# Attention with relative positions and a quantised FFN: the row maxima of four query tiles turned by one transpose, in front of the weighing matmuls

## The reference

```python
q, k, v = heads(ln(x) @ Wq + bq), heads(ln(x) @ Wk + bk), heads(ln(x) @ Wv + bv)   # (4*12, 1024, 16)
attn = einsum('bqd,bkd->bqk', q, k) / sqrt(16)
attn = attn + rel_bias_h[..., :, None] + rel_bias_w[..., None, :]   # from q and rel_h, rel_w
attn = softmax(attn, axis=-1)                                       # 1024 queries x 1024 keys
x = x + (einsum('bqk,bkd->bqd', attn, v) as (4, 32, 32, 192)) @ Wp + bp
t = x
t = t + ffn(ln(t))   # quantise, w1, gelu, clip, quantise, w2
```

## Time and profile before

| | |
|---|---|
| median of 3 runs | 863.06 us (858.8, 863.06, 864.1) |
| profiled execution | 859.48 us |
| its span, first to last instruction | 857.7 us |
| busy, share of the span | PE 90%, DVE 80%, ACT 67%, POOL 53% |
| mean granted TensorE clock | 0.951 of full speed (1.00 in the attention) |
| L1134 DVE reductions | 384, 451.5 us busy |
| L1088 ACT exponentials | 768, 410.7 us busy |
| L1013 / L993 / L1025 PE | 264.6 / 239.1 / 204.1 us busy |
| L1093 ACT copies of the maxima | 24, 24.3 us busy, 48.0 us idle before them |

### The profile page before, as it was taken

One profiled execution on the slowest core, in us unless ns is written; L12 is line 12 of the kernel. 1 busy time (PEld: TensorE's weight loads), 2 busy tenths in 40 slices (PEclk: granted clock), 3 DMA queues, 4 the chain that ended last, 5 costly groups with the idle time before them and its releaser, 6 DMA issues. The chain is left out here.

```text
span 857.7 us, 14811 instructions
## 1 busy us (share of the span) xinstructions
PE 767.9 (90%) x5688; PEld 401.1 (47%) x5688; DVE 687.9 (80%) x929; ACT 572.6 (67%) x969; POOL 453.6 (53%) x292
## 2 busy tenths in 40 slices
PE   4969565388999999999999999999999999989975
PEld 2635365244444444444444444444444444347753
DVE  6999765398888888888888888888888888249994
ACT  1233345306877887787777887787788778868773
POOL 2577699317474664837373846557473334512330
PEclk9979878659999999999999999999999999999988
DMA  7756679999959393957769492939487120033411
GB/s 196 214 165 217 207 182 372 377 210 186 190 112 209 70 216 65 217 100 163 153 125 191 88 212 66 207 66 220 92 176 140 55 82 13 13 123 128 151 37 55
DMA packets 65750, 130.02 MB, mean 152 GB/s; under 512 B 9535, under 2 KB 45392, under 8 KB 57224
## 3 DMA queue, kind: packets, MB, share of 16 engines
q1 hardware_dynamic: 57648, 115.95, 58.5%
q10 hardware_dynamic: 8032, 13.13, 4.3%
HBM read 89.73 MB, written 34.60 MB: 145 GB/s over the span
## 5 line engine op out<-in xcount | busy, mean ns | idle before, releaser
L1134 DVE TENSOR_REDUCE at_neg_max<-at_r_ps 128x1 f16<-128x1024 f32 x384 | 451.5, 1217 | 84.7 <-PE at_r_ps L993 84.7
L1088 ACT ACTIVATE at_probs<-at_s_ps 128x512 f32<-128x512 f32 x768 | 410.7, 600 | 92.8 <-PE at_s_ps L1013 92.0
L1013 PE MATMUL at_s_ps<-op_mix_q,op_mix_k 128*128 128x512 f16 x768 | 264.6, 382 | 4.6 <-ACT at_probs L1088 1.6
L993 PE MATMUL at_r_ps<-op_mix_k,op_mix_q 128*128 128x256 f16 (+1 forms) x1920 | 239.1, 257 | 16.7 <-DMA op_mix_q<-bias_parts 12.0
L1025 PE MATMUL at_o_ps<-at_probs,op_v_u 128*32 128x512 f32 x1536 | 204.1, 604 | 0.0
L993 PEld LDWEIGHTS at_r_ps<-op_mix_k,op_mix_q 128*128 128x128 f16 x1920 | 156.8, 100 | 94.1 <-DVE at_neg_max L1134 15.8
L910 POOL COPY op_mix_q<-op_mix_q 2x4096 f16<-2x4096 f16 x48 | 171.6, 3601 | 1.5
L1013 PEld LDWEIGHTS at_s_ps<-op_mix_q,op_mix_k 128*128 128x128 f16 x768 | 74.1, 97 | 166.3 <-issue 69.6
L220 POOL MEMSET op_mix_q<- 2x10240 f32 x12 | 103.5, 8627 | 21.2 <-PE at_o_ps L1025 21.1
L914 POOL TENSOR_TENSOR at_o_sb<-at_o_sb,at_inv_rows 128x512 f32<-128x512 f32 x23 | 29.4, 1280 | 126.5 <-DVE at_inv_rows L1150 125.3
L907 POOL COPY op_mix_q<-op_mix_q 2x1024 f16<-2x1024 f16 x24 | 24.9, 1036 | 107.3 <-ACT op_mix_q L1093 107.3
(11 more groups left out here) (131 smaller groups left out, 682.0 us busy)
## 6 DMA issues: line engine op xcount, KB each, us to landing
op_mix_q<-qk_parts SPq DMA_DIRECT2D x48, 640.0 KB, 11.0
op_mix_q<-bias_parts SPq DMA_DIRECT2D x120, 120.0 KB, 9.6
op_mix_q<-bias_parts SPq DMA_DIRECT2D x72, 128.0 KB, 9.5
qk_parts<-op_mix_q SPq DMA_DIRECT2D x24, 256.0 KB, 2.4
v_rows<-pr_v_st SPq DMA_DIRECT2D x8, 768.0 KB, 4.1
op_mix_k<-qk_parts SPq DMA_DIRECT2D x48, 128.0 KB, 13.3
op_v_u<-v_rows SPq DMA_DIRECT2D x12, 512.0 KB, 14.1
op_mix_q<-bias_parts SPq DMA_DIRECT2D x24, 256.0 KB, 9.7
```

The costliest lines, as they stand in the source:

```text
L993: last = pe.matmul(r_ps[count % RRING][:, first // GROUP, first % GROUP:first % GROUP + n], mix_q[owner.buf][:, variant, j, qt * P:(qt + 1 ...
L1013: pe.matmul(s_ps[use % SRING][:, :], mix_k[unit.buf][:, j, keys], mix_q[unit.buf][:, ops.VARIANT_OF[kt], j, queries], start=True, stop=Tru ...
L1088: act.activation(probs[n % PRING][:, j, :], s_ps[use % SRING][:, :], ACT.Exp).then_inc(s_taken, 1)
L1134: dve.tensor_reduce(neg_max[half][:, j // 2, t, j % 2:j % 2 + 1], r_ps[count % RRING][:, :, :].rearrange("p h t -> p (h t)"), AX_X, ALU.ma ...
```

## The change

`neg_max` gets 32 columns (SLOT) for each of the four query tiles in place of 2, of which two are written and the others are cleared once by DVE before its first reduction. One transpose then turns all four tiles of a pair of heads at once: 128 columns x 128 partitions, with tile t's two maxima in the output's partitions 32t and 32t + 1. There are two transposes for each turn, where there were eight of 2 columns each. The output is in four places, so ACT makes four copies, each of 2 partitions x 2 pairs x 128 queries, where there was one of 2 x 2 x 512. And `turn` stands at the end of step 5 and 13 (`TURN_IN`), behind that step's scores and rows and ahead of its weighing matmuls, where it stood behind them at the start of the next step.

```diff
-        neg_max = [ph.sb(f"neg_max{h}", [P, QUAD // 2, TILES, 2], F16) for h in range(2)]
+        neg_max = [ph.sb(f"neg_max{h}", [P, QUAD // 2, TILES, SLOT], F16) for h in range(2)]
...
-        TURN_AT = ((2 * KT - LEAD + 1) % STEPS, KT - LEAD + 1)
+        TURN_IN = ((2 * KT - LEAD) % STEPS, KT - LEAD)
...
         def max_rows(use):
-            return s_ps[use % SRING][:, :].bitcast(F16)[0:2, :].rearrange("p (g t) -> p g t", g=QUAD // 2)
+            return s_ps[use % SRING][:, 0:QUAD // 2 * P // 2].bitcast(F16).rearrange("p (g q) -> p g q", g=QUAD // 2)
...
                 for pair in range(QUAD // 2):
-                    for t in range(TILES):
-                        last = pe.transpose(max_rows(use)[:, pair, t * P:(t + 1) * P], neg_max[half][:, pair, t, :], ident16[:, :])
+                    last = pe.transpose(max_rows(use)[:, pair, :], neg_max[half][:, pair, :, :].rearrange("p t e -> p (t e)"), ident16[:, :])
                 last.then_inc(s_filled, 1)
...
-                    if n == TURN_AT[1]:
-                        turn(unit, 1)
-                    if n == TURN_AT[0] and not unit.last:
-                        turn(nxt, 0)
 
                     for j in range(QUAD):
                         scores(unit, n, j)
...
+                    if n == TURN_IN[1]:
+                        turn(unit, 1)
+                    if n == TURN_IN[0] and not unit.last:
+                        turn(nxt, 0)
                     if n >= LAG:
                         weigh(unit, n - LAG)
...
             def row_max_in(unit, half):
                 use = turn_use(unit, half)
                 act.wait_ge(s_filled, use + 1)
-                act.activation(mix_q[unit.buf][MAX_ROW:MAX_ROW + 2, 0, 0::2, half * GROUP:(half + 1) * GROUP],
-                               max_rows(use), ACT.Copy).then_inc(s_taken, 1)
+                rows = mix_q[unit.buf][MAX_ROW:MAX_ROW + 2, 0, 0::2, half * GROUP:(half + 1) * GROUP]
+                for t in range(TILES):
+                    last = act.activation(rows[:, :, t * P:(t + 1) * P], max_rows(use)[t * SLOT:t * SLOT + 2, :, :], ACT.Copy)
+                last.then_inc(s_taken, 1)
...
+            for half in range(2):
+                dve.memset(neg_max[half][:, :, :, :], 0.0).then_inc(neg_cleared, 1)
+            dve.wait_ge(neg_cleared, 2)
```

More of the change, by code:

```diff
@@ L837, in phase_attention @@
         s_filled, s_taken, max_spread, pv_done = (ph.sem(n) for n in ("s_filled", "s_taken", "max_spread", "pv_done"))
-        row_scored, reduced = ph.sem("row_scored"), ph.sem("reduced")
+        row_scored, reduced, neg_cleared = ph.sem("row_scored"), ph.sem("reduced"), ph.sem("neg_cleared")
         o_out, sums_turned, inv_done, inv_spread, norm_done = (
@@ L879, in phase_attention @@
             for n in range(STEPS):
-                for half in (1, 0):
-                    if n == TURN_AT[half] and (half == 1 or u + 1 < UNITS):
-                        use_of["turn", u * 2 + 1 if half else (u + 1) * 2] = len(use_of)
                 for j in range(QUAD):
                     use_of["scores", u * STEPS + n, j] = len(use_of)
+                for half in (1, 0):
+                    if n == TURN_IN[half] and (half == 1 or u + 1 < UNITS):
+                        use_of["turn", u * 2 + 1 if half else (u + 1) * 2] = len(use_of)
         def turn_use(unit, half):
@@ L889, in max_rows @@
         def max_rows(use):
-            return s_ps[use % SRING][:, :].bitcast(F16)[0:2, :].rearrange("p (g t) -> p g t", g=QUAD // 2)
+            return s_ps[use % SRING][:, 0:QUAD // 2 * P // 2].bitcast(F16).rearrange("p (g q) -> p g q", g=QUAD // 2)
         p_ps = r_ps[0][:, :, :].rearrange("p h (t c) -> p (h t) c", c=256)
-        PROJECT_FROM, PARTS = TURN_AT[1], [(t, quad) for t in range(TILES) for quad in range(NQUAD)]
+        PROJECT_FROM, PARTS = TURN_IN[1] + 1, [(t, quad) for t in range(TILES) for quad in range(NQUAD)]
         HEAD_AT = INVERT_AT[1] + 1
@@ L1033, in _ @@
             for n in range(STEPS):
-                if n == TURN_AT[0]:
-                    turn(Unit(0, 0, 0), 0)
                 for at in rows_of(n):
@@ L1038, in _ @@
                         score_row(BEFORE_FIRST, at)
+                if n == TURN_IN[0]:
+                    turn(Unit(0, 0, 0), 0)
             def emit(unit):
@@ L1107, in emit @@
                 for n in range(STEPS):
-                    if n == TURN_AT[1]:
+                    exps(unit, n)
+                    if n == TURN_IN[1]:
                         row_max_in(unit, 1)
-                    if n == TURN_AT[0] and not unit.last:
+                    if n == TURN_IN[0] and not unit.last:
                         row_max_in(unit.after(1), 0)
-                    exps(unit, n)
                     if n == O_AT[0] and not unit.first:
```

## The result

| | before | changed |
|---|---|---|
| median of 20 runs | 862.91 us (857.76 to 866.42) | 858.17 us (852.49 to 861.61) |
| ratio, 95% interval | | 0.9946 (0.9929 to 0.9964) |
| two steps with a turn | 6.41 us | 6.24 us |
| L1093 / L1094 ACT copies | 24, 24.3 us busy | 96, 35.9 us busy |
| PE busy | 767.9 us | 755.4 us |

The change gains 4.7 us, where 13.2 were forecast and 848 us stood on record with a range of 844 to 857. The direction was right; the size was not. "Two steps with a turn" is the distance between the first scores of two steps, averaged over the 21 turns that follow the first unit's first one; at any one turn the printed times give 6.23 or 6.24.

What follows compares the result with a forecast made beforehand. PE's own stream was taken to bound regular steps; a turn falling from 0.72 to 0.15 us saves 12.5 us over 22 turns, plus 0.3 and 0.4, in all 13.2. Forecast 848 us, between 846.3 and 849.9; range 844.3 to 857.

Steps and rivals of the forecast that it cites:

- What bounds: Regular steps: bound by PE's own stream at 2.84 us each; a turn adds 0.72 us, 0.43 transposes and 0.29 waiting.
- The transposes and their place: PE at the turn: two transposes before the weighing cost 0.11 us, wait for the second exponential 0 to 0.1.
- Rival 2: PE at the turn: 128-column weight loads show, 0.3 us; 9.1 us less, 850.4 to 854.0; chance 0.12.
- rival 3: PE at the turn: transposes don't stream, 0.55 us together; 4 us less, 855.5 to 859; chance 0.06.
- The copies on ACT: ACT after the fourth exponential: four copies 0.39 us each, 0.28 apart, end at 425.12; third score stalls 0.04.
- Rival 4: ACT before the next step's third score: copies become the bound; 4.3 us more, 864 to 867; chance 0.05.
- Ahead of the first unit: First turn, where DVE is the bound and idles 0.51 us behind it: most of that goes, 0.4 us gained.
- The last unit: The last unit's only turn, with no rows beside it: entered with a gain of 0.3 us.
- The base: Starting time for the gain: profiled execution 859.48 us gives 846.3, the median of runs 849.9; 848 was said.

Runs made afterwards that it cites:

- move_only: The kernel before with only the turn moved in front of the weighing, keeping eight narrow transposes and one copy: 855.48 us, ratio 0.9901.
- merge_only: Two wide transposes and four copies, but the turn left behind the weighing as in the kernel before: 870.31 us, ratio 1.007.
- one_of_four: The changed kernel with three of its four ACT copies left out: 851.71 us, ratio 0.9863.
- shapes: The changed kernel with six kinds of ACT copies by turn, differing in partitions, size or operation; turns of kind 0 take 6.24 us.
- starts: The changed kernel with six other kinds of copies by turn, varying first partitions in and out; two copies take 0.63 to 0.74 us.

## Why the prediction was wrong

*What bounds.* Right: regular steps are 2.84 us in every kernel, and a turn costs the PE's part and the wait of the third score. DVE, with its pauses gone, didn't hold up regular steps. The steps' times over 22 turns account for the medians of move_only, merge_only and one_of_four within 0.5 us.

*The transposes and their place.* Two transposes stream at 0.055 us, with 0.13 in all behind the weighing (merge_only). In front of it they cost 0.18, not 0.11. The load starts 0.11 after the second exponential ends (424.22 and 424.33), where the forecast had 0.05, and the first transpose starts 0.29 after the fourth score, where 0.21 was forecast; within the range of 0 to 0.1, and 22 x 0.07 = 1.5 us. The last unit's only turn shows that the load follows that exponential. There the exponential ends much later behind the fourth score, and the load starts 0.55 us after that score, but again 0.11 after the exponential:

```profile
725.90 2.06 ACT L1087 ACTIVATE at_probs<-at_s_ps 128x512 f32<-128x512 f32 x4 [0.67 <-PE at_s_ps L1012]
726.55 0.39 PE L1012 MATMUL at_s_ps<-op_mix_q,op_mix_k 128*128 128x512 f16 x1 [0.32 <-ACT at_probs L1087]
...
727.10 0.13 PEld L1004 LDWEIGHTS at_s_ps<-op_ident,at_neg_max 128*128 128x128 f16 x2 [0.46 <-issue]
727.13 0.27 PE L1004 MATMUL at_s_ps<-op_ident,at_neg_max 128*128 128x128 f16 x2 [0.19 <-ACT at_probs L1087]
```

What two transposes would cost at this place without the wait wasn't measured. Rival 2 (0.3 us on PE) is out, so is rival 3: the transposes stream.

*The copies on ACT: the step that failed.* The duration was right (0.373 against 0.39). The start and the distance were not. The forecast took the overlap of 0.11 us between exponentials for the copies as well, and had them end 1.72 us after the fourth exponential's start; they ended 2.16 after it. Of the 0.44, 0.14 are the late start and 0.32 the missing overlaps (3 x 0.386 against 3 x 0.28), less 0.02 for duration. The third score had no slack in the forecast, so all of it became waiting but for the 0.07 by which PE's own delay had put off the moment when the score was due: 0.36 against 0.04. Over 22 turns that is 7.0 us. one_of_four shows the cost (without three of the copies the wait is gone), and shapes and starts show why the copies don't overlap: their first partitions change from one to the next, and the first one's output begins at 96 where the exponential's begins at 0. The sign of it stood in the earlier trace rows: the copy of before ends at 425.73 and the next exponential, long ready, starts at 425.76, behind it and not 0.11 ahead.

*The rivals.* Rival 4 had the right place and was judged by a wrong point: it was asked whether a copy costs as much as an exponential's 0.49, and not whether four copies might follow each other without overlap, which needs only 0.39 each. The outcome lies between the forecast and that rival, where no case with this mechanism stood: 858.17 falls into rival 3's 855.5 to 859 by its number alone, since the transposes do stream.

*Ahead of the first unit.* The 0.4 us at the first turn can't be seen: the first unit now waits in step 5 for the loads, and so did the kernel before in its second profile. What comes earlier ahead of that point buys nothing in an execution that waits there.

*The last unit.* Its turn was entered with a gain of 0.3 us, without a working. It lost 0.1: the two steps take 5.99 us before (726.50 to 732.49) and 6.10 in the changed kernel (725.41 to 731.51), PE's own part didn't shrink there (2.92 us from step 5's first score to step 6's, 2.88 before), since the turn now waits for the second exponential, and the third score of step 6 comes 1.24 us after the first instead of 1.17.

*The base.* 859.48 was a low execution, without that wait. I went halfway between it and the median; the median (863.06, then 862.91) was the right base: 862.91 - 13.2 = 849.7, so the halving cost 1.7 us.

The ledger: 13.2 - 7.0 (copies) - 1.5 (the turn's wait) - 0.4 (first turn) - 0.4 (last unit) = 3.9 us, measured 4.7 with an interval of 3.1 to 6.1 (0.9946 of 862.91, 0.9964 and 0.9929). The forecast's 848 misses 858.17 by 10.2: 1.7 are the base and 8.5 the gain that didn't come. The terms give 9.3 for the latter, 0.8 more than the medians but within the interval. One place where the rest may lie is the first unit's first turn, which runs at the lowered clock right behind the wait: from step 5 to step 13 that unit takes 24.85 us in the changed kernel (211.32 to 236.17) and 25.91 in the second profile of before (210.92 to 236.83). That is one execution each, so it isn't shown.

## What to carry to other kernels

When one instruction is split into several, price the distance between them from a row where the same kind of operands meet, not from another loop's rhythm: a busy sum and a single duration don't tell it. Where a ring of buffers sits between two engines, write down for the next use when its buffer is free and when it is due; here the two were level in the forecast, so each mistake of the one counted in full. And a change of place and a change of shape that come together should be priced apart: here the place gave 0.33 us a turn, and the shape took back half of it until the copies were shared between two engines.

## What the runs showed of the hardware

In these traces an instruction of ScalarE that is ready starts before the end of the one ahead only if both its input and its output begin at the same partitions as those of the one ahead: then 0.09 to 0.14 us before it. Otherwise it starts 0.01 to 0.03 us after the end. Eleven kinds agree, of 2, 32 and 128 partitions, to fp16 (0.26 to 0.29 us from one to the next against 0.37 to 0.39, at 256 elements), and five of them ran after the rule was on record. The Trainium skill ("ScalarE: Activation LUTs", "What ACT_TABLE_LOAD costs") gives an overlap of 93 ns for instructions in a row. The trace agrees where the first partitions stay the same (copies of two partitions from 0 to 0 follow at 0.264 with a duration of 0.357, so 0.093), has slightly more between exponentials (0.11 to 0.12), and has none for the four copies of the changed kernel.

A transpose on PE costs about 0.055 us in a stream whether its weights have 2 or 128 columns (eight of 2 in 0.61 us, two of 128 in 0.27, the last one's 0.22 included), but at the seam it isn't the same: behind a 512-column f16 score the first one with 128 columns starts after 0.29 us, those with 2 or 64 columns after 0.31. Four transposes of 64 columns cost 0.34 us in front of the weighing and two of 128 only 0.18. Of the difference 0.11 are the two more in the stream and 0.02 the later start; the remaining 0.03 stays open.
